# Attention on one core: the order of the DMA issues in one engine's queue

## The reference

```
x = x + attention_a(layernorm(x))   # causal, 16 heads of 8; three heads weigh a third of the tokens by 1.6
x = x + ffn(layernorm(x))           # 128 -> 512 gated, two layers 512 -> 512 with gelu, 512 -> 128
x = x + attention_b(layernorm(x))   # not causal, rotary positions on q and k
x = x + ffn(layernorm(x))

scores = q @ k^T / sqrt(8);  attn = softmax(scores);  out = (attn @ v) @ W_out + b_out
```

## Time and profile before

| | |
|---|---|
| median of three runs | 2131.85 us |
| profiled execution | 2132.76 us, of which the span of the profile is 2131.0 us |
| PE, DVE, ACT, POOL busy | 91%, 81%, 69%, 52% of the span |
| causal attention, steps 3 to 17 | about 87 to 592 us |
| first feed-forward | about 592 to 980 us |
| rotary attention | about 980 to 1780 us |
| second feed-forward | to the end |
| DMA moved | 136.71 MB, mean 64 GB/s |
| mean granted clock of TensorE | 0.967 |

### The profile page before, as it was taken

The page is one execution under the profiler, slowest core; times in us unless marked ns, Lnnn a source line. Parts: engine busy times, 40 slices in busy tenths (PEclk is TensorE's granted clock), DMA queues, the critical chain, the costliest instruction groups (busy, mean ns, idle before and its releaser), DMA issues.

```text
span 2131.0 us, 43057 instructions
## 1 busy us (share of the span) xinstructions
PE 1936.5 (91%) x16196; PEld 979.3 (46%) x16196; DVE 1719.3 (81%) x2342; ACT 1480.6 (69%) x2641; POOL 1097.7 (52%) x1553
## 2 busy tenths in 40 slices
PE   3889998898889999997899999999999978999998
PEld 1333433343347777763222222222222226777776
DVE  4888887887748888876898989899898926888883
ACT  1477777776866666652688888888887875666665
POOL 5777777776545556565233333334333014555554
PEclk9899999999989999998899999999999989999999
DMA  7456665655210000012434433444444100000000
GB/s 177 96 118 127 119 128 117 125 119 112 40 47 1 1 1 1 1 32 58 86 78 86 92 73 72 85 90 87 92 79 97 23 13 12 16 11 15 11 16 16
DMA packets 106357, 136.71 MB, mean 64 GB/s; under 512 B 21153, under 2 KB 90018, under 8 KB 100002
## 3 DMA queue, kind: packets, MB, share of 16 engines
q1 hardware_dynamic: 106146, 133.89, 31.1%
HBM read 67.78 MB, written 55.58 MB: 58 GB/s over the span
## 4 chain that ended last, share of the span: by engine, by line
PE 47%; POOL 11%; SPq 11%; DMA 10%; issue 8%; DVE 8%; ACT 4%; POOLq 0%; ACTq 0%; DVEq 0%
PE ps_score L1451 20%; PE ps_out L1059 7%; PE ps_max L1451 5%; PE ps_score L1001 4%; DMA o_num<-o_raw 4%; SPq L580 4%; DVE negmax L872 3%; PE ps_max L1019 3%; DMA d_stack<-parts 3%; PE ps_out L1451 3%; ACT prob L987 2%; POOL xhat L322 2%; SPq L558 2%; PE ps_max L1100 2%; DMA stack_q<-nm_rows 2%
## 5 line engine op out<-in xcount | busy, mean ns | idle before, releaser
L987 ACT ACTIVATE prob<-ps_score 128x512 f32<-128x512 f32 x1664 | 898.9, 597 | 197.0 <-PE ps_score L1001 179.3
L872 DVE TENSOR_REDUCE negmax<-ps_max 128x2 f32<-128x1024 f32 (+1 forms) x896 | 908.0, 1065 | 136.9 <-PE ps_max L1036 73.1
L1059 PE MATMUL ps_out<-prob,v_aug 128*9 128x256 f32 (+2 forms) x6656 | 515.9, 390 | 28.2 <-ACT o_raw L950 26.0
L1451 PE MATMUL ps_score<-h,w_hi 128*128 128x512 f32 x2048 | 501.5, 398 | 10.0 <-POOL h L1223 8.2
L1451 PEld LDWEIGHTS ps_score<-h,w_hi 128*128 128x128 f32 x2048 | 381.6, 188 | 104.9 <-POOL h L1223 10.8
L1001 PE MATMUL ps_score<-stack_q,stack_k 50*128 50x512 bf16 (+3 forms) x2048 | 359.1, 351 | 56.9 <-ACT prob L987 34.4
L1019 PE MATMUL ps_max<-stack_k,stack_q 48*128 48x512 bf16 (+3 forms) x2048 | 344.7, 355 | 51.0 <-DVE negmax L872 32.4
L708 POOL TENSOR_SCALAR_AFFINE_SELECT prob<-prob 128x256 f32<-128x256 f32 (+1 forms) x448 | 188.3, 440 | 141.7 <-ACT prob L987 141.3
L1211 POOL TENSOR_TENSOR h<-h3f,h 128x512 fp32r<-128x512 f32 x128 | 192.2, 1510 | 130.9 <-ACT h L1363 130.9
L1001 PEld LDWEIGHTS ps_score<-stack_q,stack_k 50*128 50x128 bf16 x2048 | 105.3, 94 | 312.7 <-ACT prob L987 236.0
L1059 PEld LDWEIGHTS ps_out<-prob,v_aug 128*9 128x9 f32 x6656 | 106.0, 89 | 305.0 <-ACT prob L987 146.2
(11 more groups left out here) (114 smaller groups left out, 2106.9 us busy)
## 6 DMA issues: line engine op xcount, KB each, us to landing
d_stack<-parts SPq DMA_DIRECT2D x128, 192.0 KB, 2.8
stack_q<-d_stack SPq DMA_DIRECT2D x64, 384.0 KB, 5.6
stack_k<-d_stack SPq DMA_DIRECT2D x64, 384.0 KB, 6.1
d_stack<-parts SPq DMA_DIRECT2D x128, 128.0 KB, 2.8
d_stack<-parts SPq DMA_DIRECT2D x128, 64.0 KB, 2.4
o_num<-o_raw SPq DMA_DIRECT2D x128, 64.0 KB
o_rden<-d_rden SPq DMA_DIRECT2D x128, 64.0 KB
x<-in_x SPq DMA_DIRECT2D x16, 256.0 KB, 6.9
```

The costliest lines, as they stand in the source:

```text
L872: last = dve.tensor_reduce(m["negmax"][:, t, :, p], banks[:, :, at:at + w], AX.X, ALU.max, negate=True)
L987: act.activation(prob(b, i)[:, o], act_bank("score", 2 * i + o), ACT.Exp).then_inc(s["prob"], 1)
L1059: last = pe.matmul(m["ps_out"][32 * g:32 * g + HD + 1, out:out + w], m["v_aug"][b % VALUES][:, j, 4 * G + g, :], prob(b, beat)[:, g % 2, l ...
L1451: mm = pe.matmul(to, w[:, cols], moving(part), start=begin and i == 0, stop=last and i == len(pairs) - 1)
```

## The change

The body of `sync` is put in another order, and nothing else is changed. In a step, `numerators` moves to the front, then comes the second half's `aug`, and only then the load of `stack_q` (and the load of x in the causal attention). Further back the first half's `aug` moves ahead of `spread_reciprocals`.

```
@@ def sync(sp, n):
+        if on(n, 3):
+            numerators(sp, n - 3)
+        if on(n, 2):
+            aug(sp, 1, n - 2)
         if on(n, 0):
             load(sp, n, "stack_q", "stored_q", 0)
         if causal and on(n, -X_AHEAD):
             load_x(sp, m, a, n + X_AHEAD)
-        if on(n, 2):
-            aug(sp, 1, n - 2)
-        if on(n, 3):
-            numerators(sp, n - 3)
         if n > 0 and on(n, 0):
             store(sp, n, "stored_k", 1)
         if on(n, 3):
             store_reciprocals(sp, n - 3)
         if on(n, 0):
             load(sp, n, "stack_k", "stored_k", 1)
+        if on(n, 1):
+            aug(sp, 0, n - 1)
         if on(n, 3):
             spread_reciprocals(sp, n - 3)
-        if on(n, 1):
-            aug(sp, 0, n - 1)
         if on(n, -1):
             store(sp, n + 1, "stored_q", 0)
```

More of the change, by code:

```diff
@@ L613, in sync @@
             load_x(sp, m, a, n + X_AHEAD)
[L614 to L617, removed]
         if n > 0 and on(n, 0):
```

## The result

The changed kernel takes 2093.82 us (median of four runs, 2091.64 to 2096.23) against 2130.57 for the kernel before (four runs as well, one more than the three of the table above). The ratio is 0.983, with an interval of 0.981 to 0.985, so it is 1.7% faster. The forecast was 2092. The profiled execution took 2096.23 us, 36.5 less than that of before.

What follows compares the result with a forecast made beforehand. The prediction took SP's order of transfers, holding up ACT and PE in the attentions, to be on the path. Causal 28.2 plus rotary 11.7 gave 39.9 us off the profiled 2132.76, so 2092 as median, range 2072 to 2112.

Steps and rivals of the forecast that it cites:

- What bounds: SP's transfer order is on the path; the change touches four sums of attention waits, 64.0 us, and nothing outside the attentions.
- The numerators come first: In causal steps numerators issue 3.5 us earlier and land at 320.5, ending ACT's wait with a margin of 0.3 us.
- What is pushed back costs nothing: Second half's maxima rows keep 2 us to spare; `stack_q` and x are wanted later; reciprocals leave 1.4 us later, covered by POOL.
- signs of being wrong: PE waiting at beat 10 for maxima rows, POOL waiting for reciprocals before `oT`, or a causal step staying over 33 us.
- The first half's rows: Maxima rows issued 2.8 us earlier, still behind `stack_k`, cut store of k to first score from 14.1 to 12.9 us.
- less: Rival, 22%: maxima rows land no earlier because loads share DMA engines with the store of k; loop stays 32.1, time 2101.
- The causal sum: Causal step falls from 33.65 to 31.5 us; gain 28.2 us, between 15 and 45.
- two bounds that I let meet: Causal step: 31.2 down to 29.5 us without numerator wait and slow clock; 30.9 for the loop through k, up to 32.6.
- The rotary sum: Rotary attention: 9.7 us of numerator waits count fully, plus 2 of 15.4 us for maxima rows; gain 11.7 us.
- More: Rival, 20%: PE alone sets the causal step, near 30.2 us; 56 us won in all, time 2076.
- Little: Rival, 8%: numerators land 2 us later behind the store of q; only about 13 us won, time 2119.
- slower: Rival, 5%: reciprocals land 4.5 us later, costing 2 us in each of 25 steps; time about 2143.

Runs made afterwards that it cites:

- e4: The changed kernel with the load of `stack_q` moved back ahead of the numerators; 2100.23 us, 0.9845 of the kernel before.
- e5: The changed kernel with the second half's maxima rows ahead of the numerators; 2092.69 us, 0.9813 of the kernel before.
- e6: The changed kernel with a semaphore for each half of a store, each load waiting only for its own half; 2087.93 us, 0.9795 of the kernel before.
- e0: The changed kernel run again, unaltered; 2095.55 us, 0.9834 of the kernel before.
- e3: The kernel before with the new order in the causal attention only, the rotary attention keeping the old; 2109.23 us, ratio 0.9883.
- e8: The changed kernel with each load waiting only for its own half's stores and causal k's last two parts one beat later; 2091.51 us, ratio 0.9800 to before.
- e2: The kernel before with only the numerators, then the second half's maxima rows, moved ahead of the load of `stack_q`; 2117.56 us, ratio 0.9928.
- e7: The changed kernel with POOL making the last two parts of k one beat later in the causal attention; 2120.62 us, 0.9945 of the kernel before.
- e1: The kernel before with only the first half's maxima rows moved ahead of the reciprocals; 2139.51 us, ratio 1.0026.

## Why the prediction was right, point by point

**What bounds.** Right. The waits of rows 2 and 3 were the place, and only the attentions moved. That waits count by their length was too simple: 12.8 of the 19.6 us won in twelve causal steps are products at a higher clock. The prediction had this as the slow spell behind a wait, up to 1.7 us a step.

**The numerators come first.** Right, to a few tenths. SP goes on when the fourth group is copied; the landing takes as long as before (e4); the causal wait fell from 33.5 to 2.1 us where I had allowed 8, and no full step has a wait left. The last wait, in step 17, stayed as said, and became 2.1 instead of 0.9.

**What is pushed back costs nothing.** Right for the second half's rows (e5), for x, and for `stack_q` as far as the rows show (see the next point). For the reciprocals one of my signs of being wrong did come, without a cost: POOL stood still before `oT` for 0.43 us in one rotary step, and for 15.9 us where the rotary pipeline drains. There the reciprocals do not leave 1.4 us later. They stand behind maxima rows that are not ready, and go 17.3 us after the store of k, where it was 7.0. POOL's next work comes 20.5 us after its last before this wait, before and after the change.

**The first half's rows: 12.9 us from the store of k to the first score.** This is the step that failed. In no causal step of the pipeline's middle is it under 13.2 us; over the twelve steps it is 13.2 to 14.5. Three rows after the change, the last from the rotary part, and one of before to hold against it:

```profile
252.77 3.89 SPq L580 DMA_DIRECT2D d_stack<-parts  x6
265.99 0.12 PEld L1001 LDWEIGHTS ps_score<-stack_q,stack_k 50*128 50x128 bf16 x2 [0.18 <-DMA stack_q<-nm_rows]
...
1411.16 0.12 PEld L1001 LDWEIGHTS ps_score<-stack_q,stack_k 50*128 50x128 bf16 x2 [0.99 <-issue]
```

```profile
1486.84 0.13 PEld L1001 LDWEIGHTS ps_score<-stack_q,stack_k 50*128 50x128 bf16 x2 [0.99 <-DMA stack_q<-nm_rows]
```

In e6 the load goes a microsecond earlier and the interval is still 13.2 (283.76 to 296.99). So this is not the time of the rows but the work of PE and ACT between the two. Rotary step 1, from which I had 12.9, is at the start of the pipeline and holds less of that work; there e6 does shorten the interval, to 11.2. In the rotary part it is 14.4 us before (1472.40 to 1486.84) and after (1396.71 to 1411.16), and PEld stands still 0.99 us in both. Only the releaser's name has changed. That the rows cannot pass the load holds all the same, but by their landings (last section) and not by the 1.2 us that I had taken for it. What holds PE at the head of causal steps is `stack_k` itself, which lands last, up to 14.1 us after the store of k began (315.74 to 329.84).

Why it lands so late in those steps is open. In that step the load went 7.15 us after the store's first issue, against 5.8 in most, because the store had landed later. The rival "less" had put such a thing down to the load of `stack_q` ahead of the store, but this load stands 7.4 to 7.8 us ahead in all of the twelve steps, the quick ones too, and before the change, with 11 to 15 us between them, the load of `stack_k` went as late as 7.69 us after the store's first issue. These waits cost 6.4 us in all, and e6 shows that 6 to 8 us could be had back at this place.

**The causal sum.** Forecast a step of 31.5 and 28 us. Measured 31.96, 31.70 and 32.04 in three profiles (the change, e0, e3), and 25 us by the runs of e3. Right within its bounds, but not for the reason given. The leg of 18.0 us is what it was in nine of the twelve steps, 18.0 to 18.1. With the other leg at 13.2 the step has a floor of 31.2, and e6 stays there with the load out of the way and the clock at 1.00. The floor is the work of PE, ACT and POOL (with POOL's masks out of PE's way, e8 goes under it), and not the loop through k by way of the rows. Of the two bounds that I let meet, the upper end of the first, 31.2, was the true one, and 30.9 for the second was too short.

**The rotary sum.** Mis-sized: 11.7 us forecast, 17.3 measured. The step fell from 46.20 to 45.05, 13.8 us over twelve steps; the rest lies in the steps at the two ends, which I had not counted. The 2 us for the maxima rows are what they bring there (0.2 a step, e2 against the change), and the guess that PE would spend about 1.0 of each such wait in any case is what the 0.99 above shows. The term that was too small is the 9.7 us for the numerators: they brought 0.95 us a step, 11.4 over the twelve, and most of the 3.5 us at the ends. A wait of ACT in rows 11 made its step longer by 1.22 for each us of it, and I had rounded that factor down to one.

**The sum of both.** That 2092 came so near to 2093.82 is partly luck: the causal term was 3 us too high by the runs of e3 and 8.6 by the profile, and the rotary one 5.6 too low.

**The rivals.** "More" did not come: in e6's twelve steps the wait at the head is gone and the clock is 1.00, and its step is 31.44, not 30.2. "Less" came in small part, as waits for `stack_k`. "Little" and "slower" did not come. A theory of mine that fell is not in the prediction but behind it: that the two halves of the change add up.

## What to carry to other kernels

When an in-order queue of DMA issues holds up two places, try the changes for both together before judging either: here the one alone read as a small loss, the other as under half of the gain. Put what is ready first and short ahead of what is large and waits for a landing, and look at where SP stands still rather than at how busy the DMA engines are. Before a wait is judged by its length, see what TensorE's granted clock does behind it: here waits of 1.5 us on average on ACT were mostly absorbed (e4), and 12 us more of waits on PE, with the lower clock behind them, cost 25 (e7). And before a wait that names a DMA is counted, look whether the engine goes on any sooner where the name is gone.

## What the runs showed of the hardware

- The landing of four 64 KB transfers from eight partitions each took 6.6 us from the first issue with nothing ahead of them (rows 8). With 768 KB (e4) or 1 MB of loads (before) ahead it was 6.9 in the step shown; over all causal sequences of these two kernels and the change it is 6.4 to 7.2.
- The maxima rows that are issued directly behind the load of `stack_k` land with it: in the change 0.3 us before to 0.6 us after its last part, by the landings that the trace records.
- Idle stretches of PE at the heads of the causal steps of 2.0 us on average (e7) went with a granted clock of 0.95, of 1.15 us (e8) with 0.98, and none (e6) with 1.00:

```profile
100.00:530.00 430.00, 398.65 (x5488) 176.44 (x5484) 385.98 (x543) 347.49 (x660) 335.32 (x680) 1.00 0.65 124
```

- What stays open: whether the lower clock alone makes e1 slower than before. PE's 3.8 us more of busy time go with it, but no run here held the clock and changed the wait. Open too is why a store of k lands later in some steps, so that the load behind it goes at 7.15 us (7.69 before) and not at 5.8.
